# A hybrid attention and FFN kernel: head dims laid four abreast, so that one pack copy fills two groups, and one pool of pack slots for both attentions

## The reference

```
x = x + attn_a(ln(x))   # 16 heads of 16 dims; softmax over |i-j| <= 32 or i < 4 or j < 4
x = x + ffn(ln(x))      # silu(x Wg) * (x Wu) Wd, hidden 768, int weights / 127
x = x + attn_b(ln(x))   # exp(rope(q) rope(k)) / sum exp(q k), then causal mask, 16 heads of 16
x = x + ffn(ln(x))
```

## Time and profile before

| | |
|---|---|
| median of 3 runs | 2284.94 us (2279.85 to 2287.68) |
| the profiled execution's own time | 2286.64 us |
| its span, first to last instruction | 2284.9 us |
| mean granted TensorE clock | 0.929 |
| PE busy | 1942.2 us, 85% |
| DVE busy | 1400.6 us, 61% |
| ACT busy | 1447.9 us, 63% |
| DMA queue q1 (all of SP's) | 129344 packets, 197.80 MB, 36.3% of 16 engines |

### The profile page before, as it was taken

One profiled execution on the slowest core, in us unless ns is written; L12 is line 12 of the kernel. 1 busy time (PEld: TensorE's weight loads), 2 busy tenths in 40 slices (PEclk: granted clock), 3 DMA queues, 4 the chain that ended last, 5 costly groups with the idle time before them and its releaser, 6 DMA issues.

```text
span 2284.9 us, 63345 instructions
## 1 busy us (share of the span) xinstructions
PE 1942.2 (85%) x25221; PEld 1397.1 (61%) x25221; DVE 1400.6 (61%) x2971; ACT 1447.9 (63%) x3580; POOL 785.3 (34%) x1131
## 2 busy tenths in 40 slices
PE   5677889899897989989898988989899898979785
PEld 4463657566675756667575666757566675756445
DVE  5363657576675757567575756757575675755533
ACT  1228676676767666676766667675666767667480
POOL 0023233334334333433433343343334334334331
PEclk7688989999999999999999999999999999999887
DMA  6214343342434334243433424343342434333221
GB/s 186 71 42 97 61 119 83 93 95 75 108 73 110 81 99 96 75 102 75 106 80 99 97 73 102 73 111 78 99 95 77 101 72 112 79 91 93 60 63 33
DMA packets 129637, 201.87 MB, mean 88 GB/s; under 512 B 26769, under 2 KB 60561, under 8 KB 129313
## 3 DMA queue, kind: packets, MB, share of 16 engines
q1 hardware_dynamic: 129344, 197.80, 36.3%
HBM read 67.87 MB, written 51.52 MB: 52 GB/s over the span
## 4 chain that ended last, share of the span: by engine, by line
PE 58%; ACT 14%; DVE 11%; DMA 7%; issue 4%; SPq 4%; POOL 1%; ACTq 0%; POOLq 0%; DVEq 0%
PE gu_bank L1051 15%; PE d_bank L1067 7%; PE gu_bank L1079 6%; PE gu_bank L1015 5%; ACT s_bank L1165 5%; DMA xn<-o_scr_B 4%; PE s_bank L982 4%; PE s_bank L946 4%; ACT probs_B L1155 3%; SPq L574 3%; PE gu_bank L1025 3%; PE s_bank L812 2%; PE s_bank L967 2%; DVE xn L1372 2%; DMA o_scr_B<-o_raw 2%
## 5 line engine op out<-in xcount | busy, mean ns | idle before, releaser
L1165 ACT ACTIVATE s_bank<-s_bank 128x512 f32<-128x512 f32 x1024 | 602.6, 591 | 191.6 <-PE s_bank L946 190.8
L1574 POOL TENSOR_TENSOR h<-tmp,h 128x512 fp32r<-128x512 f32 x192 | 252.0, 1312 | 458.7 <-DVE h L1455 458.7
L1155 ACT ACTIVATE probs_B<-s_bank 128x512 f32<-128x512 f32 x640 | 334.5, 609 | 46.0 <-PE s_bank L967 43.2
L1051 PE MATMUL gu_bank<-xT,w_g 128*128 128x256 f32 x1536 | 238.2, 300 | 25.6 <-DVE tmp L1438 23.4
L1051 PEld LDWEIGHTS gu_bank<-xT,w_g 128*128 128x128 f32 x1536 | 211.1, 201 | 52.8 <-DVE tmp L1438 37.2
L1051 PE MATMUL gu_bank<-xT,w_u 128*128 128x256 f32 x1536 | 240.3, 297 | 2.7 <-DVE tmp L1444 0.5
L1194 ACT ACTIVATE tmp<-gu_bank 128x512 f32<-128x512 f32 x192 | 114.4, 596 | 197.2 <-PE gu_bank L1051 189.6
L1051 PEld LDWEIGHTS gu_bank<-xT,w_u 128*128 128x128 f32 x1536 | 208.1, 198 | 35.7 <-issue 20.4
L1438 DVE SCALAR_TENSOR_TENSOR tmp<-tmp,gu_bank 128x512 f32<-128x512 f32 x192 | 130.9, 682 | 159.5 <-ACT tmp L1194 158.1
L1067 PE MATMUL d_bank<-w_d,h 128*128 128x256 f32 x1536 | 225.3, 289 | 3.3 <-POOL h L1574 3.3
L946 PE MATMUL s_bank<-pack_b 48*128 48x512 f16 x1024 | 184.6, 406 | 45.8 <-DMA pack_b<-src_b 30.9
(11 more groups left out here) (140 smaller groups left out, 3288.0 us busy)
## 6 DMA issues: line engine op xcount, KB each, us to landing
pack_b<-src_b SPq DMA_DIRECT2D x768, 64.0 KB, 2.4
pack_a<-src_a SPq DMA_DIRECT2D x384, 64.0 KB, 2.3
x<-in_L_attn_a_x_dram SPq DMA_DIRECT2D x32, 512.0 KB, 4.7
o_scr_A<-o_raw SPq DMA_DIRECT2D x64, 256.0 KB, 2.4
o_scr_B<-o_raw SPq DMA_DIRECT2D x64, 256.0 KB, 2.4
xn<-o_scr_A SPq DMA_DIRECT2D x32, 256.0 KB
rden_on<-r_scr_A SPq DMA_DIRECT2D x32, 256.0 KB
x_scr<-x SPq DMA_DIRECT2D x16, 512.0 KB, 2.8
```

Of the source, the lines that this page charges most:

```text
L1051: last = pe.matmul(bank[:, f * D:(f + 1) * D], plain(w[:, k, c:c + P], exact), plain(given[:, k, half * D:(half + 1) * D], exact), start=k ...
L1155: act.activation(probs["B"][:, i, :], score_bank("NP", n // 2, q, n % 2)[:, :], ACT.Exp, scale=SM_SCALE)\
L1165: act.activation(bank[:, :], bank[:, :], ACT.Exp, scale=SM_SCALE, accum_out=den[:, 0, j, 2 * tile + e, t:t + 1]).then_inc(den_exp, 1)
L1574: pool.tensor_tensor(h[1][:, i % 2, :], tmp[:, i % 2, :], h[0][:, i % 2, :].bitcast(F32), ALU.subtract)\
```

## The change

The columns of the q and k weights are reordered when they are split, so that in every 64 partitions of src_a and src_b the 16 dims of 4 heads lie abreast: partition 64 b + 4 r + h is dim r of head 4 b + h (ABREAST = 4). The rope tables, the matrix that swaps neighbouring dims, the head selectors and the bias loads follow. A copy of every second partition (first + e, step 2, 32 of them) then holds one head of each of two groups, and lands in 16 partitions of a slot for two groups: 128 KB with 2 KB source runs. So a pair of groups takes six copies, a sequence 36. UL, RL and SL keep two places each (SL 372, 381; UL 1026, 1121; RL 1075, 1170), and PE waits once for each pair.

pack_a and pack_b become one tensor of the same size, packs, with 2 x 2 double slots. Attention a of sequence q uses side q % 2, both; pair p of b uses side (q + p) % 2, slot 0 plain, slot 1 rotated. What frees a slot changes accordingly: SL(0) and SL(1) wait for the first pair of b of sequence q - 2, UL(1) and RL(1) for attention a of sequence q + 1. The fill of the maxima rows is done for each side (the second one ahead of SL(0) of sequence 1).

```diff
+PAIRS, ABREAST = GROUPS // 2, 4
+
+
 def head(j, c):
 
     return HEADS // 2 * (c // 2) + 2 * j + c % 2
+
+
+def heads_abreast(a):
+
+    return a.rearrange("p (b h r) -> p b r h", h=ABREAST, r=DH)
+
+
+def dims_abreast(a):
+
+    return a.rearrange("p (b r h) -> p b r h", h=ABREAST, r=DH)
...
-    "UL": (1026, 1062, 1121, 1224),
-    "RL": (1075, 1128, 1170, 1278),
+    "UL": (1026, 1121),
+    "RL": (1075, 1170),
...
-    "SL": (372, 381, 388, 389),
+    "SL": (372, 381),
...
-        pack_a = sb("pack_a", [P, GROUPS, 2, KT, S], F16)
-        pack_b = sb("pack_b", [P, 2, 2, 2, KT, S], F16)
+        packs = sb("packs", [P, 2, 2, 2, 2, KT, S], F16)
...
-                sp.dma_start(qk_bias[:, 2 * n:2 * n + 2], b.rearrange("(t p) -> p t", p=P),
-                             allow_slow_non_contiguous=True).then_inc(c_in, 16)
+                for half in range(KT * PAIRS):
+                    t, side = divmod(half, PAIRS)
+                    first = ABREAST * DH * side
+                    rows = bass.AP(tensor=b.tensor, offset=b.offset + ABREAST * DH * half, ap=[[1, DH], [DH, ABREAST]])
+                    sp.dma_start(qk_bias[first:first + ABREAST * DH, 2 * n + t:2 * n + t + 1], rows,
+                                 allow_slow_non_contiguous=True).then_inc(c_in, 16)
...
+            def fill_maxima_rows(side):
+                for e in range(2):
+                    rows = packs[HB * e + ROWS:HB * e + HB, side, :, :, :, :, :].rearrange("p a j q t s -> p (a j) (q t s)")
+                    sp.dma_start(rows, a_fill_in[e]).then_inc(fills_in, 16)
+
+            fill_maxima_rows(0)
+
+            def load_pack(dst, given, pair, packed):
 
                 for n, (q, k) in enumerate(zip(Q_PARTS, K_PARTS)):
                     for e in range(2):
-                        rows = given[2 * DH * j + DH * e:2 * DH * j + DH * e + DH, 0, q, :, :]
+                        first = ABREAST * DH * pair
+                        rows = given[first + e:first + ABREAST * DH:2, 0, q, :, :]
                         size = KT * S
                         rows = bass.AP(tensor=rows.tensor, offset=rows.offset,
                                        ap=[list(rows.ap[0]), [(2 + k - q) * size, 2], [1, size]])
                         r = HB * e + DH * n
-                        sp.dma_start(dst[r:r + DH].rearrange("p q t s -> p q (t s)"), rows).then_inc(packed, 16)
-
-            def load_a(j, q):
-                if j == 0:
+                        sp.dma_start(dst[r:r + DH].rearrange("p j q t s -> p j q (t s)"), rows).then_inc(packed, 16)
+
+            def load_a(pair, q):
+                if pair == 0:
                     sp.wait_ge(gu_taken, gu_use("T", 3, "PA", q) + 1)
-                if q:
-                    sp.wait_ge(a_scores, (q - 1) * UNITS["A"] + 2 + 4 * (j + 1))
-                load_pack(pack_a[:, j], src_a, j, a_packed[j])
-
-            def load_b(rotated, j, q):
+                if q == 1 and pair == 0:
+                    sp.wait_ge(wb_split, 1)
+                    fill_maxima_rows(1)
+                elif q > 1 and pair == 0:
+                    sp.wait_ge(den_scores, (q - 2) * UNITS["D"] + UNITS["D"] // PAIRS)
+                elif q > 1:
+                    sp.wait_ge(b_scores, (q - 2) * UNITS["N"] + UNITS["N"] // PAIRS)
+                load_pack(packs[:, q % 2, pair], src_a, pair, a_packed[pair])
+
+            def load_b(rotated, pair, q):
+                if pair == 0 and rotated:
+                    sp.wait_ge(rot_ready, (q + 1) * 4)
+                elif pair == 0:
+                    sp.wait_ge(gu_taken, gu_use("T", 3, "PB", q) + 1)
                 scores, units = ((den_scores, UNITS["D"]), (b_scores, UNITS["N"]))[rotated]
-                if j == 0 and rotated:
-                    sp.wait_ge(rot_ready, (q + 1) * 4)
-                elif j == 0:
-                    sp.wait_ge(gu_taken, gu_use("T", 3, "PB", q) + 1)
-                if j >= 2:
-                    sp.wait_ge(scores, q * units + units // GROUPS * (j - 1))
-                elif q:
-                    sp.wait_ge(scores, (q - 1) * units + units // GROUPS * (j + 3))
-                elif j == 0 and not rotated:
-                    sp.wait_ge(wb_split, 1)
-                load_pack(pack_b[:, j % 2, rotated], src_b[:, rotated], j, (u_packed, r_packed)[rotated][j])
+                if pair == 0 and q:
+                    sp.wait_ge(scores, q * units)
+                elif pair == 0:
+                    sp.wait_ge(a_scores, 2 + 8 * (rotated + 1))
+                elif q < SEQS - 1:
+                    sp.wait_ge(a_scores, (q + 1) * UNITS["A"] + 2 + 8 * (rotated + 1))
+                else:
+                    sp.wait_ge(scores, (q - 1) * units + units // PAIRS)
+                load_pack(packs[:, (q + pair) % 2, rotated], src_b[:, rotated], pair, (u_packed, r_packed)[rotated][pair])
...
-                    if kind == "A1" and p % 2:
-                        pe.wait_ge(a_packed[p // 2], (q + 1) * 96)
+                    if kind == "A1" and p == 1 and q < 2:
+                        pe.wait_ge(fills_in, (48, 80)[q])
+                    if kind == "A1" and p % 4 == 1:
+                        pe.wait_ge(a_packed[p // 4], (q + 1) * 96)
...
-                if n % 8 == 0:
-                    pe.wait_ge(u_packed[j], (q + 1) * 96)
+                if n % 16 == 0:
+                    pe.wait_ge(u_packed[j // 2], (q + 1) * 96)
...
-                if n == 0:
-                    pe.wait_ge(r_packed[j], (q + 1) * 96)
+                if n == 0 and j % 2 == 0:
+                    pe.wait_ge(r_packed[j // 2], (q + 1) * 96)
...
-                w, c = ((wa_qk, 0), (wa_qk, D), (wa_v, 0), (wa_o, 0))[n]
-                split([a[:, :, c:c + D] for a in w], bank).then_inc(w_taken, 1)
+                if n < 2:
+                    for k in range(KT):
+                        last = split([dims_abreast(a[:, k, n * D:(n + 1) * D]) for a in wa_qk], heads_abreast(bank[:, k, :]))
+                else:
+                    last = split([a[:, :, :] for a in (wa_v, wa_o)[n - 2]], bank)
+                last.then_inc(w_taken, 1)
...
-                split([w[:, :, :] for w in wb_qk], st_bqkv[:, :, 0:2 * D])
+                for k in range(KT):
+                    split([dims_abreast(w[:, k, :]) for w in wb_qk], heads_abreast(st_bqkv[:, k, 0:2 * D]))
...
-    d = np.arange(P) % DH
+    d = np.arange(P) // ABREAST % DH
```

More of the change, by code:

```diff
@@ L415, in build @@
         prep = sem("prep")
-        a_packed = [sem(f"a_packed{j}") for j in range(GROUPS)]
-        u_packed = [sem(f"u_packed{j}") for j in range(GROUPS)]
-        r_packed = [sem(f"r_packed{j}") for j in range(GROUPS)]
+        a_packed = [sem(f"a_packed{j}") for j in range(PAIRS)]
+        u_packed = [sem(f"u_packed{j}") for j in range(PAIRS)]
+        r_packed = [sem(f"r_packed{j}") for j in range(PAIRS)]
         pair_open = sem("pair_open")
@@ L490, in stage @@
             return a.rearrange(f"p ({' '.join(names)}) -> p {' '.join(names)}", **dict(zip(names, shape)))
-        st_b = pack_b[:, :, :, :, :, :].rearrange("p a b c d s -> p (a b c d s)").bitcast(F32)
-        st_a = pack_a[:, :, :, :, :].rearrange("p a b c s -> p (a b c s)").bitcast(F32)
+        st_b = packs[:, 1, :, :, :, :, :].rearrange("p a b c d s -> p (a b c d s)").bitcast(F32)
+        st_a = packs[:, 0, :, :, :, :, :].rearrange("p a b c d s -> p (a b c d s)").bitcast(F32)
         st_probs = probs["A"][:, :, :].rearrange("p a b -> p (a b)")
@@ L560, in _ @@
             sp.wait_ge(w_flag, 3)
-            for e in range(2):
-                rows = pack_a[HB * e + ROWS:HB * e + HB, :, :, :, :].rearrange("p j q t s -> p j (q t s)")
-                sp.dma_start(rows, a_fill_in[e]).then_inc(fills_in, 16)
-            def load_pack(dst, given, j, packed):
+            def fill_maxima_rows(side):
[4 more added lines that the diff above has]
+            def load_pack(dst, given, pair, packed):
                 for n, (q, k) in enumerate(zip(Q_PARTS, K_PARTS)):
                     for e in range(2):
-                        rows = given[2 * DH * j + DH * e:2 * DH * j + DH * e + DH, 0, q, :, :]
+                        first = ABREAST * DH * pair
+                        rows = given[first + e:first + ABREAST * DH:2, 0, q, :, :]
                         size = KT * S
@@ L597, in load_maxima @@
             def load_maxima(q):
-                if q == 0:
-                    sp.wait_ge(fills_in, 48)
+                if q < 2:
+                    sp.wait_ge(fills_in, (48, 80)[q])
                 sp.wait_ge(ntopT_ready, q + 1)
@@ L605, in load_maxima @@
                             first = HEADS * n + HEADS // 2 * tile
-                            sp.dma_start(pack_a[row:row + 1, :, 0, tile, :], ntopT[first + e:first + HEADS // 2:2, :]).then_inc(ntop_in, 16)
+                            rows = packs[row:row + 1, q % 2, :, :, 0, tile, :].rearrange("p a j s -> p (a j) s")
```

(9 more changed lines are left out.)

11 lines of the change are left out of this document (5 added, 6 removed).

## The result

| | before | after |
|---|---|---|
| median of 4 runs each | 2286.31 us (2279.85 to 2288.19) | 2326.18 us (2321.73 to 2331.97) |
| ratio | | 1.0189, 95% interval 1.0161 to 1.0218 |
| span of the profiled execution | 2284.9 us | 2320.0 us (the fastest of the four) |
| mean granted TensorE clock | 0.929 | 0.923 |

The change makes the kernel 1.9% slower, 40 us. The prediction was 2286 us with a range up to 2312, so it was wrong; the rival "write side of 16 partitions binds", with 2332 us and a chance of 0.10, was near.

A forecast was written before the change was run, and what follows sets the result against it. The prediction took PE's matmul list, stalled by attention b's output round trip (BO(3), OL), as the bound. It summed -4.3 + 2.5 - 0.7 + 0.6 + 3.0 = +1.1 us to a 2286 us median, range 2269 to 2312.

The forecast's parts named there:

- write side of 16 partitions binds: Pack copies into 16 partitions run at 115 GB/s, +2.9 us ahead of each BO(3); 2332 us, chance 0.10.
- The bytes of UL(0): UL(0)'s copies double to 128 KB, so BO(3) queued behind them lands later: 0.6 us a turn.
- The path: In full turns BO(3) or OL delays PE one for one; O's stall covers DP(0)'s wait growing under 3.31 us.
- one of the signs of being wrong that I had named: The forecast would be wrong if the PE clock falls after the longer stalls at DP(0); no size given.
- UL(1)'s absence: Behind OL, UL(1) no longer competes with xn's loads: at most 0.68 us a turn back, 0.4 taken.
- Sequence 0: At the start, fewer copy issues bring packs earlier and DVE's last maxima end near 60.0 us: gain 4.3 us.
- the eight small bias loads: Eight instead of two, so SP's later constant loads start 2 to 14 us later; likely 4 us, covered, cost nothing.
- Sequence 1: Side 1's fill ahead of the first packs makes PE stand 1.6 to 4.6 us; with later relief, +2.5 us.
- The slots: New waits of SL, UL and RL for freed slots are over by the list's own order: cost nothing.
- the issue time: SP issues a pack copy in 0.60 us as before, since the new pattern's extra dims fold: no cost.
- the pattern rival: The deeper copy pattern costs 0.26 us more issue each, 1.6 us ahead of BO(3): 2309 us, chance 0.06.

The follow-up runs named there:

- copies_step: Copies alone, computation left out, 128 KB into 16 partitions, destination step varied: step 1 8.5 us a group, steps 2, 3, 4, 8 5.65, 5.85, 5.45, 5.65.
- rot_early: The changed kernel with the last swap product and the rotation's last two roundings moved ahead of DP's exponentials: 2306.18 us, ratio 1.0106.
- w_early: The changed kernel with only the last swap product of the rotation, W(3), moved from place 1037 to 1033: 2319.16 us, ratio 1.0161.
- fill_early: The changed kernel with the fill of side 1 issued right behind the packs of sequence 0: 2328.05 us, ratio 1.0186.
- apart: The changed kernel with only the joining undone, twelve groups of six 64 KB copies at the places of before: 2294.75 us, ratio 1.0039.
- before_spread: The kernel before with only the pack rows interleaved, so each 64 KB copy writes 16 partitions three apart: 2267.70 us, ratio 0.9936.
- apart_spread: The changed kernel with the joining undone (twelve groups of six 64 KB copies) and pack rows interleaved: 2270.89 us, ratio 0.9936.

## Why the prediction was wrong

**The bytes of UL(0): the step that failed.** I took 0.6 us a turn, from 0.33 to 0.41 us of engine time for a copy, spread over 16 engines. Measured, a group of the new form takes +2.9 us alone, and from UL(0)'s first issue to DP(0) +2.0 on average of 15 sequences (8.6 against 6.6; 9.0 against 6.8 in the turn shown). BO(3) behind it, for which I had the 0.6, lands after 4.93 us on average of 15 turns instead of 2.71: +2.2. And DP(0)'s waits are 62.3 us in total, where I had written some 40. The share of busy engines didn't tell whether six copies into 16 neighbours can use them all. The row for it was there: the fill's 115 GB/s at a share of 0.90. I held against the write-side rival that 64 KB copies were already faster than that rate. That was the false argument: alone they take 5.5 us, of which 3.8 are issuing, and 5.15 with spread rows, so they sat near what the writes allow, and the double ones are set by it. Windows of after (columns as above), while UL(0) is under way and while SL's twelve copies are issued: in both the core moves 119 GB/s, at shares of 0.73 and 0.84.

```profile
1112.88:1121.80 8.92, 4.92 (x164) 2.60 (x156) 3.15 (x5) 3.44 (x7) 6.03 (x5) 0.87 0.73 119
1173.42:1181.10 7.68, 6.33 (x53) 5.23 (x52) 6.29 (x10) 4.39 (x12) 3.19 (x4) 1.00 0.84 119
```

The Trainium skill (SBUF — State Buffer, "Door 1: The DMA port swizzle") says that 16 neighbouring partitions reach 4 of 16 ports. By that rule a step of 2 or more reaches more of them, and copies_step agrees: 8.5 us against 5.45 to 5.85. Its figure for such a copy is 109 GB/s; the windows show 119, with the other transfers of the core in it. One difference that the runs show the rule doesn't give: 32 neighbouring partitions took 6.5 to 6.65 us, sixteen with a step of 2 took 5.65.

**The path.** I said that BO(3), OL and O carry a delay one for one and that DP(0)'s wait is covered by O's stall while it grows by less than 3.31 us. In the turn shown it grew by 2.2, and O's stall of 3.31 went altogether, because the list between the two also got 1.9 us longer (10.05 us against 8.14 without the stall), in part by the clock of 0.50 behind DP(0)'s longer stall; that is one of the signs of being wrong that I had named. BO(3)'s own +2.2 was hidden behind this. On average of 15 turns O starts 18.6 us after UL(0)'s first issue, 18.1 before: so a turn loses 0.5 us up to O, and the other 1.4 behind it, where NP(0) stands. What I missed is who else waits behind DP(0): ACT's last rounding, then RL(0), whose own copies are slow as well. I let NP(0) have no wait at all; it has 45.0 us, more than the turns lose, as DP(0)'s growth (+31.4) and O's relief (-42.6) nearly cancel. rot_early showed the link, w_early excluded the cheaper one.

**UL(1)'s absence.** I took 0.4 us a turn. The loads of xn do land sooner, 0.8 us: from OL's first issue to DVE's first use it takes 6.1 us instead of 6.95 on average of 15 turns. But O hardly binds in the change, so it gave next to nothing there. With quick copies O's wait is 27 us smaller joined (31.6 against 58.7), but 20 of these stand at DP(0) and NP(0) instead: net 7.5 us in the whole span, 0.5 a turn. That is near what I took, but by luck: it holds all that joining does, and not this term alone.

**Sequence 0**, -4.3 us: it was 0. The second pair's issue came early as I said, but pair 0 landed 4.5 us later. Of these 3.2 are its own landing, 9.25 us from the first issue instead of 6.02: that term was wrong. The other 1.3 is a later first issue (43.38 against 42.09). I put it down to the eight small bias loads and what follows, which I held covered; no run has them alone.

**Sequence 1**, +2.5 us: first near scores +7.4, transposes behind them +9.1. The fill is 4.1 of it by the stall and 4.9 by the time of the near scores (fill_early), at the upper end of my bounds of 1.6 to 4.6 or just over; slow copies make the rest.

**The slots, the issue time.** As predicted: no slot is late, and the issue of a copy stays 0.600 us, so the pattern rival fell. (The store that I compared with, 0.336 us, is that of attention a; BO, the one that counts here, has a median of 0.504.) apart gives what the rest of the change costs without joining, 0.4%.

**The rival's number.** 2332 us against 2326. Its cause was right, and BO(3) did get 2.2 us later where it had 2.5, but the path was another: a turn lost 1.9 us, at DP(0) and NP(0), and the start lost more than the rival said. That the sum came so near is partly luck.

## What to carry to other kernels

When copies are joined, look at which partitions each one writes before counting bytes and issues: a group of six 128 KB copies into 16 neighbours cost 8.5 us, with a step of 2, 3, 4 or 8 under 6. Where the order of rows is free, as in a contraction, try interleaving them; here that one line was worth 0.6% without the joining, and with it the joined kernel with the early fill is 1.5% faster than the kernel before, of which some 0.7% is the joining. And when a stall moves, follow every queue behind the instruction that now stands, not only the one that the old stall was on.

## What the runs showed of the hardware

The share of busy engines and the time to land are different things. With 64 KB copies the queue's share is 36.3% (before) and 36.4% (before_spread), where a copy reads 16 neighbouring partitions, and 26.6% (apart) and 25.9% (apart_spread), where it reads every fourth; the landings are 2.4, 2.4, 2.6 and 2.1 us. So for these copies the share goes by where they read, and hardly tells the landing. With 128 KB copies slow writes raise the share too (40.5% against 27.9%).

In the kernel before and in before_spread a turn takes 129.2 to 130.7 us where the granted clock is 0.99 on average, and 132.4 to 133.9 where it fell to 0.50 for some us (0.95 to 0.97 on average). Behind stalls of PE of 3.3 us at O (before) and of 4.08 and 3.22 us at DP(0) and NP(0) (after) it did fall. Whether a shorter stall would hold it, and so count for more than its length, no run here shows.
